# First attention with scores computed once, third attention with stacked queries

## The reference

```python
q = (query @ Wq).reshape(b, sq, 32, 16)    # 32 query heads of 16
k = (key @ Wk).reshape(b, sk, 8, 16)       # 8 key heads, each for 4 query heads
scores = einsum('bhqd,bhkd->bhqk', q, k) / 4
out = einsum('bhqk,bhkd->bhqd', softmax(scores), v) @ Wo
```

## Time and profile before

| | us |
|---|---|
| median of 3 runs | 1655.13 (1654.13 to 1655.79) |
| the profiled execution, its own time | 1655.96 |
| its span, first to last instruction | 1654.2 |
| PE busy in the span | 1477.4 (89%) |
| VectorE busy | 981.1 (59%) |
| ScalarE busy | 547.8 (33%) |
| GpSimd busy | 531.9 (32%) |

### The profile page before, as it was taken

The page is one execution under the profiler, slowest core; times in us unless marked ns, Lnnn a source line. Parts: engine busy times, 40 slices in busy tenths (PEclk is TensorE's granted clock), DMA queues, the critical chain, the costliest instruction groups (busy, mean ns, idle before and its releaser), DMA issues.

```text
span 1654.2 us, 20269 instructions
## 1 busy us (share of the span) xinstructions
PE 1477.4 (89%) x6854; PEld 1055.1 (64%) x6854; DVE 981.1 (59%) x2158; ACT 547.8 (33%) x1414; POOL 531.9 (32%) x531
## 2 busy tenths in 40 slices
PE   0788888877888989999899998899999999999898
PEld 0344444434766677676678776777777777777555
DVE  2565666655768334888322245677777777777543
ACT  1223222233342213454323113334434334434332
POOL 4100000004523232341312113545545545443163
PEclk9999999999999979999899999999999999999799
DMA  5111111112313210010111104111111111110001
GB/s 157 53 39 37 33 32 33 28 36 90 96 58 102 64 51 1 8 33 1 39 39 51 39 1 147 32 58 51 46 58 51 46 58 51 46 48 4 7 1 51
DMA packets 63481, 77.52 MB, mean 47 GB/s; under 512 B 7138, under 2 KB 34018, under 8 KB 63252
## 3 DMA queue, kind: packets, MB, share of 16 engines
q1 hardware_dynamic: 62416, 74.99, 14.9%
q10 hardware_dynamic: 964, 1.25, 0.2%
HBM read 57.34 MB, written 10.49 MB: 41 GB/s over the span
## 4 chain that ended last, share of the span: by engine, by line
PE 70%; DVE 12%; issue 5%; POOL 4%; SPq 4%; DMA 3%; ACT 2%; POOLq 0%; DVEq 0%; ACTq 0%
PE bank L423 15%; PE bank L428 14%; PE bank L427 14%; SPq L910 3%; PE bank L2331 3%; PE bank L1961 2%; PE bank L2309 2%; PE bank L1950 2%; PE bank L2224 2%; DMA ring_l<-k 2%; PE bank L1959 2%; PE bank L2206 2%; PE bank L490 1%; DVE xn L1807 1%; PE bank L2318 1%
## 5 line engine op out<-in xcount | busy, mean ns | idle before, releaser
L1012 POOL TENSOR_TENSOR ring_l<-stage,ring_h 128x512 fp32r<-128x512 f32 x133 | 179.0, 1363 | 235.6 <-ACT ring_h L1168 235.6
L423 PE MATMUL bank<-xTh_b,ring_h 128*128 128x512 f32 x464 | 191.3, 412 | 2.8 <-issue 1.5
L427 PE MATMUL bank<-xTl_b,ring_h 128*128 128x512 f32 x464 | 185.4, 400 | 0.0
L428 PE MATMUL bank<-xTh_b,ring_l 128*128 128x512 f32 x464 | 185.2, 399 | 0.0
L1119 POOL TENSOR_TENSOR q<-xn 128x512 f32<-128x512 f32 x64 | 82.2, 1284 | 220.6 <-DVE xn L1807 220.6
L423 PE MATMUL bank<-ring_h,o3h 128*128 128x512 f32 x256 | 125.7, 491 | 0.8 <-issue 0.8
L1446 ACT ACTIVATE probs<-bank,nbias 128x128 f32<-128x128 f32 x256 | 90.5, 366 | 54.7 <-DVE nbias L1831 54.7
L1437 ACT ACTIVATE probsT<-bank 128x512 f32<-128x512 f32 x64 | 38.3, 598 | 205.6 <-PE bank L2318 205.6
L423 PEld LDWEIGHTS bank<-xTh_b,ring_h 128*128 128x128 f32 x464 | 88.8, 191 | 23.2 <-issue 4.4
L428 PEld LDWEIGHTS bank<-xTh_b,ring_l 128*128 128x128 f32 x464 | 88.5, 191 | 21.7
L428 PE MATMUL bank<-ring_h,o3l 128*128 128x512 f32 x256 | 101.0, 395 | 0.0
(11 more groups left out here) (327 smaller groups left out, 3535.0 us busy)
## 6 DMA issues: line engine op xcount, KB each, us to landing
stage<-in_units_dram SPq DMA_DIRECT2D x133, 256.0 KB, 3.2
ring_h<-q SPq DMA_DIRECT2D x64, 64.0 KB, 2.0
ring_l<-k SPq DMA_DIRECT2D x64, 64.0 KB, 2.1
raw_k<-kvs SPq DMA_DIRECT2D x16, 256.0 KB, 2.1
raw_v<-kvs SPq DMA_DIRECT2D x16, 256.0 KB, 2.0
kraw<-raw_k SPq DMA_DIRECT2D x16, 256.0 KB, 3.4
v<-raw_v SPq DMA_DIRECT2D x16, 256.0 KB, 3.0
stage<-in_context_dram SPq DMA_DIRECT2D x8, 256.0 KB, 3.1
```

The source lines that it names most:

```text
L423: ins = nc.tensor.matmul(out_ap, wh, mh, start=start, stop=False)
L427: nc.tensor.matmul(out_ap, wh, ml, start=False, stop=False)
L428: return nc.tensor.matmul(out_ap, wl, mh, start=False, stop=stop)
L1012: nc.gpsimd.tensor_tensor(ring_l[:, place_of(u), :], stage[:, u % STAGE, :], f32(ring_h[:, place_of(u), :]), ALU.subtract).then_inc(w_lo, 1)
```

## The change

The first attention computes its scores once, negated (`queries0` of ACT now has scale -1, the mask constant its other sign). DVE takes the row minimum. In even turns DVE subtracts it (into `probs`), in odd turns ACT does, in four pieces. PE transposes the four 128x128 tiles with four matmuls against the identity, and ACT takes the exponential with a negative or positive scale. `q0b`, its memset, its transfers, `pick4`, `block4`, `mB`, `mhl`, `mraw`, `maximum0`, `halves0`, `turned_max0`, `blocks_of_max0` and `turned_scores0` go. The loop goes by turn instead of by group: 68 steps, each with the scores of turn l, the transposes of turn l-2 and the outputs of turn l-3.

The third attention puts the high queries of a set of heads on partitions 0 to 63 and the low ones on 64 to 127 (`qs`), copies the block-diagonal keys by DMA from the half that holds them to the other, and so needs two matmuls of 512 columns a turn instead of three. ACT does the subtraction in every second turn. Both splits of the queries are now two instructions of 64 partitions in place of one of 128. Some semaphores are merged.

```diff
 # constants: pick4 and block4 go, rep is half as wide (8*P columns)
-            nc.sync.dma_start(block4[:, :, :], d["block4"]).then_inc(s_rep, 16)
-            nc.gpsimd.memset(q0b.bitcast(F32), 0.0).then_inc(su_zero, 1)
 # SP, first attention
             for g in range(G0):
-                sp.wait_ge(a0_ev, at0(g, "q"))
-                if g >= 2:
-                    sp.wait_ge(a0_st, 4 * (g - 2) + 4)
-                blocks0(q0b, q0[:, g % 2, :], g, s_q0b)
                 sp.wait_ge(a0_ev, at0(g, "k"))
...
 # SP, third attention
+            for gr in range(16):
+                b, s = gr // 2, gr % 2
+                own, other, heads = slice(64 * s, 64 * s + 64), slice(64 - 64 * s, P - 64 * s), slice(4 * s, 4 * s + 4)
+                sp.wait_ge(a2_kb, gr + 2)
+                nc.sync.dma_start(f32(kb2[other, :, b % 2, heads, :]), f32(kb2[own, :, b % 2, heads, :])).then_inc(s_kd[gr % 4], 16)
+                if gr >= 3:
+                    load.upto(U_L2F + min(gr - 2, 6))
 # ACT, first attention
+            def lessened0(n):
+                a.wait_ge(a0_mx, n // 2 + 1)
+                if n >= 3:
+                    a.wait_ge(a0_tr, n - 2)
+                for h in range(4):
+                    c = slice(h * P, (h + 1) * P)
+                    ins = nc.scalar.activation(probs[:, n % 3, c], bank[n % 2][:, c], ACT.Identity, scale=-1.0,
+                                               bias=nbias[:, n % 4, h:h + 1])
+                ins.then_inc(a0_sa, 1)
+            for l in range(4 * G0 + 4):
+                g, p = l // 4, l % 4
+                if 2 <= l < 4 * G0 + 2:
+                    exponentials0(l - 2)
+                if l < 4 * G0 and on_act0(l):
+                    lessened0(l)
+                if p == 3 and g >= 1:
+                    outputs0(g - 1)
+                if p == 0 and g + 1 < G0:
+                    queries0(g + 1)
+                if p == 1 and g + 1 < G0:
+                    keys0(g + 1)
...
 # DVE, first attention
+            def least0(n):
+                v.wait_ge(a0_s, n + 1)
+                rows4 = by_tile(bank[n % 2][:])
+                if on_act0(n):
...
+                    nc.vector.tensor_reduce(nbias[:, n % 4, :], rows4, AX.X, ALU.min).then_inc(a0_mx, 1)
+                    return
+                link(v, v_chain, nc.vector.tensor_reduce(nbias[:, n % 4, :], rows4, AX.X, ALU.min))
...
+                nc.vector.tensor_tensor(by_tile(probs[:, n % 3, :]), rows4, nbias[:, n % 4, :].unsqueeze(2).to_broadcast((P, 4, P)),
+                                        ALU.subtract).then_inc(a0_sd, 1)
+            for l in range(4 * G0 + 4):
+                g, p = l // 4, l % 4
+                if l < 4 * G0:
+                    least0(l)
+                if p == 1 and g >= 2:
+                    normalized0(g - 2)
+                if p == 3 and g % 2 == 0 and g + 2 < G0:
+                    low_qk0((g + 2) // 2)
+                top(1 if p == 3 else 2)
...
 # PE, first attention
+            def turned0(n):
+                ready0(t, n)
+                if n >= 2:
+                    t.wait_ge(a0_e, n - 1)
+                for h in range(4):
+                    c = slice(h * P, (h + 1) * P)
+                    ins = nc.tensor.transpose(bank[2 + n % 2][:, c], probs[:, n % 3, c], ident[:, :])
+                ins.then_inc(a0_tr, 1)
+            for l in range(4 * G0 + 3):
+                g, p = l // 4, l % 4
+                if l < 4 * G0:
+                    scores0(g, p)
+                if 2 <= l < 4 * G0 + 2:
+                    turned0(l - 2)
+                if p == 0 and g >= 2:
+                    turned_outputs0(g - 2)
+                if l >= 3:
+                    outputs0((l - 3) // 4, (l - 3) % 4)
+                if p == 0 and g + 1 < G0:
+                    queries0(g + 1)
+                if p == 1 and g + 1 < G0:
+                    keys0(g + 1)
+                if p == 2 and g % 2 and g + 1 < G0:
+                    values0((g + 1) // 2)
+                if p == 2 and g % 2 == 0 and g + 2 < G0:
+                    projection0((g + 2) // 2)
 # third attention: ACT and DVE write qs in two halves, PE
-                mm3(bank[n % 2][:], qh[:, r, cols2(b)], ql[:, r, cols2(b)], kbh[:, b % 2, 4 * s:4 * s + 4, :],
-                    kbl[:, b % 2, 4 * s:4 * s + 4, :], True, True).then_inc(a2_s, 1)
+                q, heads = qs[:, s, r, cols2(b)], slice(4 * s, 4 * s + 4)
+                ins = nc.tensor.matmul(bank[n % 2][:], q, kbh[:, b % 2, heads, :], start=True, stop=False)
...
+                nc.tensor.matmul(bank[n % 2][:], q, kbl[:, b % 2, heads, :], start=False, stop=True).then_inc(a2_s, 1)
```

More of the change, by code:

```diff
@@ L542, in program, with on_act0, ready0 @@
         G0 = 2 * B
+        def on_act0(n):
+            return n % 2 == 1
+        def ready0(eng, n):
+            eng.wait_ge(a0_sa if on_act0(n) else a0_sd, n // 2 + 1)
         def at0(g, kind):
@@ L792, in program @@
         a2_ql = sem("a2_ql")
-        a2_z = sem("a2_z")
         a2_kb = sem("a2_kb")
+        s_kd = [sem(f"s_kd{i}") for i in range(4)]
         a2_s = sem("a2_s")
@@ L809, in lessened2 @@
         def lessened2(t, count):
[L811 to L813 removed]
+            t.wait_ge(a2_sb, count - count // 2)
+            if count >= 2:
+                t.wait_ge(a2_sa, count // 2)
         def pair2(j):
@@ L1206, in queries0 @@
                     a.wait_ge(a0_s, 4 * (g - 2) + 4)
-                    a.wait_ge(s_q0b[g % 2], 64 * (g // 2))
-                nc.scalar.activation(q0[:, g % 2, :], bank[7][:], ACT.Identity, bias=col(C_ONE)).then_inc(a0_ev, 1)
+                nc.scalar.activation(q0[:, g % 2, :], bank[7][:], ACT.Identity, bias=col(C_ONE), scale=-1.0).then_inc(a0_ev, 1)
             def keys0(g):
@@ L1266, in _, with exponentials0 @@
-            outputs0(G0 - 1)
+            def exponentials0(n):
+                at = 4 * (n // 8) + n % 4
+                a.wait_ge(a0_tr, n + 1)
+                if n >= 3:
+                    a.wait_ge(a0_pv, n - 2)
+                nc.scalar.activation(probsT[:, n % 3, :], bank[2 + n % 2][:], ACT.Exp, bias=bcol[:, at:at + 1],
+                                     scale=(scol if on_act0(n) else scol_n)[:, at:at + 1]).then_inc(a0_e, 1)
+            def lessened0(n):
+                a.wait_ge(a0_mx, n // 2 + 1)
+                if n >= 3:
+                    a.wait_ge(a0_tr, n - 2)
[4 more added lines that the diff above has]
+                ins.then_inc(a0_sa, 1)
@@ L1353, in _ @@
                 c = slice(i // 4 * HALF, (i // 4 + 1) * HALF)
-                nc.scalar.activation(qh[:, i % 4, c], bank[i % 2][:], ACT.Copy, scale=-0.25).then_inc(a2_qh, 1)
+                for s in range(2):
+                    ins = nc.scalar.activation(qs[0:64, s, i % 4, c], bank[i % 2][64 * s:64 * s + 64, :], ACT.Copy, scale=-0.25)
+                ins.then_inc(a2_qh, 1)
             for half in range(2):
                 nc.scalar.activation(kh2[:, half * HALF:(half + 1) * HALF], bank[4 + half][:], ACT.Copy).then_inc(a2_qh, 1)
-            a.wait_ge(a2_z, 1)
+            a.wait_ge(a2_kb, 1)
             for half in range(2):
@@ L1381, in _ @@
                     nc.scalar.activation(pair2(j)[:, m % 2, :], bank[2 + m % 2][:], ACT.Exp,
-                                         scale=1.0 if m % 4 == 3 else -1.0).then_inc(a2_e, 1)
-                if l % 4 == 3 and l < N2:
+                                         scale=1.0 if m % 2 else -1.0).then_inc(a2_e, 1)
+                if l % 2 and l < N2:
                     less_on_act2(l)
```

203 lines of the change are left out of this document (57 added, 146 removed).

## The result

The changed kernel takes 1542.8 us (median of four runs, 1538.5 to 1543.7) against 1655.4 before: the ratio is 0.9313, 95% interval 0.9301 to 0.9325. A second set of runs of the same kernel gave 1539.5 and 0.9308 (0.9295 to 0.9321). The forecast was 1589, with a range from 1572 to 1622: the sign was right, the size was not. The profiled execution took 1542.79 with a span of 1541.0, which is 113.2 less than the span before.

A forecast was written before the change was run, and what follows sets the result against it. PE was taken to bound both attentions, the first at the lower clock. Terms: -6.5 start, -60 first loop, +2.5 and -7 third attention, +4 clock, sum -67; 1655.96 - 67 = 1589 us, 8-in-10 range 1572 to 1622.

The forecast's parts named there:

- So 15.0 us a group: First attention, loop: PE's 14.3 us a group plus 0.6 waiting for `pvs`; 242 us against 301.7, so -60.
- the table of costs: First attention, loop: PE's matmul costs by turn at the lower clock, sum 14.3 us for a group of four turns.
- rival 2: First attention gets the higher clock, VectorE bounds: 12.9 us a group instead of 15.0, -34, 1555 us; chance 0.08.
- Two signs: First attention: forecast is wrong if PE waits for key blocks each group, or if VectorE is busy without pause.
- The argument against rival 2: First attention: PE was busy 250.5 of 296 us and never rose, and 512-column matmuls become fewer.
- The rule on transposes: Skill page: transposes don't count as PE being busy for the clock; cited against rival 2; by it alone 1670 us.
- VectorE's 12.4 us: First attention, loop: VectorE's work per group of four turns, 12.4 us, below PE's 14.3.
- The keys' wait: First attention, loop: new keys take 5.3 us while PE has 6.4 of work, hidden with 1.1 us to spare.
- The start: Before the first attention's loop: memset of `q0b`, query issues and queue load go; -6.5 us (-4.8 to -7.3).
- Third attention: +2.5 us before its loop, -7 in the loop (7.9 us a group), +4 for the clock.
- the fall of the clock at its first scores: Third attention: PE's new gap drops the clock, first ten turns about 3 us instead of 1.9; +4 us (0 to +20).
- The -75 bound: First attention, loop: no wait at all and 14.3 us a group gives -75 us.

The follow-up runs named there:

- e10: Changed kernel with two unused 32-row matmuls of 512 columns added in each turn of the first attention; 1602.6 us (executions between 1575 and 1650), ratio 0.9582.
- e7: Changed kernel with all four subtractions of a group of the first attention on VectorE, none on ACT; 1556.9 us, ratio 0.941.
- e8: Changed kernel with three of four subtractions of a group of the first attention on ACT; 1529.8 us, ratio 0.9249.
- e5: e3 with the matmul of the maxima over 128 rows, of which 96 are zero, instead of 32; 1591.5 us, ratio 0.9614.
- e9: e3 with four more 128x128 transposes in each turn of the first attention, their results overwritten; 1656.6 us, ratio 0.9988.
- r16: Changed kernel with each turn's four transposes of logits replaced by one 128-row matmul of constants in the first attention; 1548.3 us, ratio 0.9362.
- e6: Changed kernel with one unused 32-row matmul of 512 columns ahead of each turn's scores in the first attention; 1561.8 us, ratio 0.944.
- e11: e8 with keys made in turn 0, queries in turn 1, and outputs turned one turn later; 1522.2 us, ratio 0.9195.
- e2: Kernel before with only the third attention's part of the change; 1654.8 us, ratio 0.9994.
- e3: Kernel before with each group's key blocks issued ahead of its query blocks in the first attention; 1645.1 us, ratio 0.9931.
- e12: e11 with all four subtractions of a group of the first attention on ACT; 1509.8 us, ratio 0.9117.

## Why the prediction was wrong

- **The step that failed** is "So 15.0 us a group" in the loop of the first attention: PE as the bound, at 1.2 GHz throughout. It forecast -60 us; the loop lost 104.6. The work was counted rightly: e10's low stretch, which is this loop with two matmuls more a turn, has 21.0 us a group, and the table of costs gives 14.3 + 4 x (0.72 + 0.72 + 0.13) = 20.6. What was wrong was to take the lower level as a property of the place. 14.3 us a group is what PE would need if it never rose; it rose at about 63 us and was up for two thirds of the window from 60 to 200, and VectorE set 12.3 us a group (197.0 / 16; e7 and e8 show the bound). That is rival 2, which had 0.08; it came to 12.3 where I had 12.9. Two signs that the prediction names for being wrong came: PE waited for the keys in 14 groups of 16, and VectorE was busy almost without pause.
- **The argument against rival 2** was that PE had been busy 250.5 of 296 us and never rose, and that 512-column matmuls become fewer. e5 shows what stood behind the first half: the 32-row matmul of the maxima, with a load that shows at each change between 32 and 128 rows. I had the row in hand, took the 0.29 us a piece as time, and did not ask what its absence does to the clock. The second half was wrong as well: fewer wide matmuls, but four transposes a turn for them, and e9 and r16 show that these count. How much of the rise in the changed kernel comes from each stays open: e6 puts one 32-row matmul a turn back and the clock stays up, e10 puts two back and it comes down for half of the loop, r16 takes the transposes out and it is up less.
- **The rule on transposes.** e9 rises with transposes added and r16 rises less with them removed, so the rule from the Trainium skill, page "TensorE: Matmul & The Clock Gate", section "Part 4: PE-mode transpose", does not hold for these transposes of 4-byte values; the measurement decides. The section speaks of matmuls in a transpose mode; the traces list these as plain matmuls against the identity, and whether they run in that mode no trace here shows. I had doubted the rule ("No row above isolates it"), but it still pressed on the chance of rival 2.
- **VectorE's 12.4 us** a group was 11.7 (132.8 of 140 us busy, times 12.3): right within 6%. The keys' wait, which I had hidden with 1.1 us to spare at 1.2 GHz, is 22.6 us because PE comes round earlier; it costs little while VectorE bounds, and e11, which moves the keys and `pvs`, got 5.1 us of loop for both.
- **The start** was right to 0.7 us: the memset is gone, `iota` lands at 20.9 instead of 22.2. **Third attention**: +3.4 before its loop (+2.5), the period 7.76 us (7.9), the fall of the clock at its first scores as foreseen (granted 0.61 in 540 to 550 us) but over after 9 us, +1.4 instead of +4. No run undid these one by one; they are read from the trace, so how well single terms came out may be luck. The sum for the third attention is -4.0 in the trace; with the 1.9 that is given back behind it -2.1, which lies inside the interval of e2 (-2.5 to +0.5).
- **The range** began at 1572, half of rival 2. With the level open, its lower end belonged at rival 2 in full, 1555, and below: 1542.8 lies under even that. The -75 bound that the prediction names beside it gives 1574.

The chain of waits in the third attention's loop, which answers to the earlier trace rows: from one reciprocal of VectorE to the next is one period, 7.76 us.

```profile
599.12 0.57 issue
599.69 1.76 DVE rs L1734
...
607.45 1.76 DVE rs L1734
```

## What to carry to other kernels

When a stage runs at the lower clock with PE seemingly busy, look at the distance between starts and find which loads show before taking the level as given. Here giving a small matmul all 128 rows, 96 of them zero, was worth 53.6 us (e5 against e3). Forecast such a stage twice, at both levels, with the second engine's load as the floor, and give the higher level a real chance whenever the change removes what thins PE's work. And once an engine other than PE bounds, small moves off that engine pay nearly in full: two such moves (e8, e12) and one change of order (e11) gave 33 us.

## What the runs showed of the hardware

- At 1.2 GHz a 512-column matmul next to one with another number of rows (128 and 32) starts 0.72 us after it (e3) instead of 0.43 (e5); at 2.4 GHz it is 0.42 (e9) instead of 0.23 (e5). The Trainium skill, page "TensorE: Matmul & The Clock Gate", section "Step-by-step: what each phase is for", says that the weight load is pulled ahead when the row groups don't conflict or it goes to the background buffer; the 0.43 of e5 at 1.2 GHz is what a load that is pulled ahead would give, and the 0.72 of e3 what one that isn't would. Why a change of rows should prevent it no run here isolates.
- The same instructions can run at either level with PE busy all the time: e10 ran its loop for 135 us at 1.2 GHz and then for almost 90 mostly at 2.4 (185 to 274 us), and its executions differ by 75 us. What decides at which moment it rises stays open.
- Matmuls with 96 of 128 rows zero are no slower than over 32 rows, and the clock rose with them where it had not with the 32-row form (e5 against e3).
- The granted clock reads 1.00 until the first logged change, which comes at 398 us in the kernel before; until then only the durations tell (793 ns for a 512-column matmul at 1.2 GHz, some 390 to 500 at 2.4).
